# First context block in halves ahead of the tokens, and the last sums of the first attention placed ahead of other steps

## The reference

```
x = x + L0_xattn(layernorm(x), ctx)     # the setup and the first attention
x = x + L0_ffn(layernorm(x))            # shared experts and top 2 of 8
x = x + L1_xattn(layernorm(x), ctx)
x = x + L1_ffn(layernorm(x))

L0_xattn(q_feat, kv):                   # HIDDEN = 128
  Q = q_feat @ Wq;  K = kv @ Wk;  V = kv @ Wv
  ctx = softmax(Q K^T / sqrt(128)) @ V
  out = ctx @ Wo + bo + q_feat
  out = out @ Wfc
  return layernorm(out) * gamma + beta
```

## Time and profile before

| | us |
|---|---|
| median of 3 runs | 1042.13 (1041.17 to 1043.61) |
| profiled execution | 1041.9 |
| its span | 1040.1 |

### The profile page before, as it was taken

One profiled execution on the slowest core, in us unless ns is written; L12 is line 12 of the kernel. 1 busy time (PEld: TensorE's weight loads), 2 busy tenths in 40 slices (PEclk: granted clock), 3 DMA queues, 4 the chain that ended last, 5 costly groups with the idle time before them and its releaser, 6 DMA issues. The chain is left out here.

```text
span 1040.1 us, 18454 instructions
## 1 busy us (share of the span) xinstructions
PE 985.0 (95%) x6808; PEld 907.8 (87%) x6808; DVE 685.7 (66%) x1629; ACT 511.5 (49%) x1044; POOL 403.6 (39%) x631
## 2 busy tenths in 40 slices
PE   6999999699899999989989999999999999999996
PEld 5899998588899999988778889999998999999985
DVE  7577787568588888765675454455445676677664
ACT  5446666432477777753435333333334444444442
POOL 5514445507233443415632000000014767768651
PEclk9999999999999999999999999999999999999997
DMA  7200000101388888824213300000000111101000
GB/s 231 82 1 1 1 2 1 62 21 62 125 292 261 262 257 254 256 85 127 64 52 122 72 1 21 2 1 1 2 1 11 26 26 32 32 21 27 21 11 16
DMA packets 56878, 76.51 MB, mean 74 GB/s; under 512 B 5536, under 2 KB 37408, under 8 KB 56800
## 3 DMA queue, kind: packets, MB, share of 16 engines
q1 hardware_dynamic: 40480, 51.61, 16.0%
q0 software_dynamic: 15648, 22.81, 7.6%
q10 hardware_dynamic: 672, 1.05, 0.3%
HBM read 61.43 MB, written 14.02 MB: 73 GB/s over the span
## 5 line engine op out<-in xcount | busy, mean ns | idle before, releaser
L2472 DVE TENSOR_TENSOR XT_lo<-bank,XT_lo 128x512 fp32r<-128x512 f32 x116 | 73.3, 633 | 79.0 <-ACT XT_lo L2132 79.0
L43 PE MATMUL bank<-V_hi,XT_lo 128*128 128x256 f32 x416 | 123.6, 297 | 1.2 <-DVE XT_lo L2472 1.2
L2132 ACT ACTIVATE XT_lo<-bank 128x512 fp32r<-128x512 f32 x116 | 63.9, 553 | 120.1 <-PE bank L1839 119.5
L45 PE MATMUL bank<-V_hi,XT_lo 128*128 128x256 f32 x416 | 117.2, 282 | 0.0
L44 PE MATMUL bank<-V_lo,XT_lo 128*128 128x256 f32 x416 | 116.9, 281 | 0.0
L2477 DVE TENSOR_REDUCE part<-wide 128x1 f32<-128x402 f32 (+1 forms) x116 | 72.4, 624 | 39.7 <-PE wide L45 37.8
L43 PE MATMUL wide<-expert_w_hi,XT_hi 128*128 128x402 f32 (+2 forms) x236 | 93.5, 396 | 4.3 <-issue 2.4
L45 PE MATMUL wide<-expert_w_hi,XT_hi 128*128 128x402 f32 (+2 forms) x236 | 87.6, 371 | 0.0
L44 PE MATMUL wide<-expert_w_lo,XT_hi 128*128 128x402 f32 (+2 forms) x236 | 87.3, 370 | 0.0
L43 PEld LDWEIGHTS bank<-V_hi,XT_lo 128*128 128x128 f32 x416 | 78.3, 188 | 4.6 <-DVE XT_lo L2472 2.9
L44 PEld LDWEIGHTS bank<-V_lo,XT_lo 128*128 128x128 f32 x416 | 78.9, 190 | 0.4
(11 more groups left out here) (499 smaller groups left out, 3270.8 us busy)
## 6 DMA issues: line engine op xcount, KB each, us to landing
sraw<-w1T SPq DMA_DIRECT2D x13, 512.0 KB, 5.1
sraw<-w3T SPq DMA_DIRECT2D x13, 512.0 KB, 5.1
sraw<-w2T SPq DMA_DIRECT2D x13, 512.0 KB, 5.5
sraw_odd<-w1T SPq DMA_DIRECT2D x12, 512.0 KB, 4.8
sraw_odd<-w3T SPq DMA_DIRECT2D x12, 512.0 KB, 5.0
sraw_odd<-w2T SPq DMA_DIRECT2D x12, 512.0 KB, 5.1
XT_hi<-queries POOLq DMA_DIRECT2D x16, 256.0 KB, 3.2
routed_results<-rys POOLq DMA_DIRECT2D x15, 256.0 KB, 4.8
```

The costliest lines, as they stand in the source:

```text
L43: pe.matmul(out, wh, xh, start=first, stop=False)
L45: return pe.matmul(out, wl, xh, start=False, stop=last)
L2132: act.activation(weights(g, nk, 0), transposed(g, nk), ACT.Copy).then_inc(sem["high"], 1)
L2472: dve.tensor_tensor(weights(g, nk, 1), transposed(g, nk), weights(g, nk, 0).bitcast(F32), ALU.subtract).then_inc(sem["low"], 1)
```

## The change

In the setup the first context block is loaded, made into a high and a low part and multiplied in two halves of 256 columns. Both halves are issued by ACT, ahead of tokens 0, and the load of the whole block is gone from SP. On DVE the low parts of the weights and of the two halves now stand ahead of `statistics(0)`, and `statistics(1)` stands behind `normalise(0)` and the low part of `Wq`. In the first attention `split(14)` stands on POOL ahead of the second `inverse(12)`, and, for the tile step i = 15, `finish(13)` on DVE ahead of the statistics of tile 11's residual.

```diff
@@ first attention, POOL
                     for i in range(3, nq + 2):
-                        split(i - 3)
+                        if i <= nq:
+                            split(i - 3)
                         if real(i - 4):
                             add(i - 4)
                         inverse(i - 3, MV, RSTD, SHIFT, stat1, inv1)
+                        if i == nq:
+                            split(LAST - 1)
                         if real(i - 4):
                             inverse(i - 4, MV2, R2, H2, stat2, inv2)
@@ first attention, DVE
+                        if i == LAST:
+                            finish(i - 2)
                         if real(i - 4):
                             partial(i - 4, X, residual, stat2)
-                        if real(i - 2):
+                        if real(i - 2) and i < LAST:
                             finish(i - 2)
@@ setup, SP
                     weight("L0_xattn_Wv", lda)
-                    context(0)
                     weight("L0_xattn_Wq", ldq)
@@ setup, ACT
                 def _(act):
+                    for h, sem in enumerate((ldc_first, ldc[0])):
+                        act.dma_start(ctf[:, :, first_half(h)], A["ctxT"].rearrange("(c p) n -> p c n", p=P)[:, :, first_half(h)])\
+                           .then_inc(sem, 16)
                     act.dma_start(X[:, 0:4 * D].rearrange("p (i d) -> p i d", d=D),
...
-                    context_high(0)
+                    for h, sem in enumerate((ldc_first, ldc[0])):
+                        act.wait_ge(sem, 16)
+                        act.activation(CT_hi[:, :, first_half(h)], ctf[:, :, first_half(h)], ACT.Copy).then_inc(ctx_high, 1)
                     normalise(0)
@@ setup, DVE
+                    first_weights(0, slice(nq, na))
+                    for h in range(2):
+                        x = first_half(h)
+                        dve.wait_ge(ctx_high, h + 1)
+                        dve.tensor_tensor(CT_lo[:, :, x], ctf[:, :, x], CT_hi[:, :, x].bitcast(F32), ALU.subtract).then_inc(ctx_low0, 1)
                     statistics(0)
-                    first_weights(0, slice(nq, na))
-                    context_low(dve, 0)
-                    statistics(1)
                     normalise(0)
                     first_weights(1, slice(0, nq))
+                    statistics(1)
                     low(0)
@@ setup, PE
+                            if b == 0:
+                                for h in range(2):
+                                    pe.wait_ge(ctx_low0, h + 1)
+                                    x = first_half(h)
+                                    for c in range(DC):
+                                        m = mm3(pe, bank[:, x], kh[:, c, :], kl[:, c, :], CT_hi[:, c, x], CT_lo[:, c, x],
+                                                h == 0 and c == 0, h == 1 and c == DC - 1)
```

More of the change, by code:

```diff
@@ L2813, in build @@
                 ldc = sems(ctx, "ldc0 ldc1 ldc2 ldc3")
+                (ldc_first,) = sems(ctx, "ldc_first")
                 (first_high, first_low, second_high, second_low, ctx_high, ctx_low0, ctx_low, fold_high, fold_low, folded, fold_kept,
@@ L2855, in context_low, with first_half @@
                     x = ctx_cols(b)
-                    eng.wait_ge(ctx_high, b + 1)
-                    eng.tensor_tensor(CT_lo[:, :, x], ctf[:, :, x], CT_hi[:, :, x].bitcast(F32), ALU.subtract)\
-                       .then_inc(ctx_low if b else ctx_low0, 1)
+                    eng.wait_ge(ctx_high, b + 2)
+                    eng.tensor_tensor(CT_lo[:, :, x], ctf[:, :, x], CT_hi[:, :, x].bitcast(F32), ALU.subtract).then_inc(ctx_low, 1)
+                def first_half(h):
+                    return slice(256 * h, 256 * h + 256)
                 @blk.sync
@@ L3095, in unit @@
                         elif kind == "k":
-                            if b:
-                                pe.wait_ge(ctx_low, b)
[L3098 to L3103, removed]
+                            if b == 0:
[5 more added lines that the diff above has]
+                                                h == 0 and c == 0, h == 1 and c == DC - 1)
+                            else:
+                                pe.wait_ge(ctx_low, b)
+                                x = ctx_cols(b)
+                                for c in range(DC):
+                                    m = mm3(pe, bank[:, 0:x.stop - x.start], kh[:, c, :], kl[:, c, :], CT_hi[:, c, x], CT_lo[:, c, x],
+                                            c == 0, c == DC - 1)
                         elif kind == "v":
```

## The result

| | before | after |
|---|---|---|
| median of 20 runs | 1041.62 us (1038.54 to 1045.23) | 1045.67 us (1042.95 to 1051.3) |
| profiled execution | 1041.9 | 1043.3 |
| its span | 1040.1 | 1041.5 |
| first score matmul (the setup's end) | 41.84 | 46.92 |
| first waiting matmul of the experts | 206.84 | 211.38 |

The changed kernel is slower: the ratio is 1.0049, with a 95% interval of 1.0035 to 1.0062, or 3.6 to 6.5 us. I had forecast 1043.5 and no change that can be told. The median, 1045.67, lies just outside the range given, and within 0.6 us of the rival in which the clock stays low, 1045.1.

What follows compares the result with a forecast made beforehand. TensorE, busy 95% of the span, was taken as the bound. Setup + 2.2, split - 0.9 and finish(13) + 0.1 gave + 1.4 us: 1043.5 for the median, range 1041.3 to 1045.6.

Steps and rivals of the forecast that it cites:

- the rival in which the clock stays low: Setup, turn(0) to turn(1): PE stays at the low rate, costing 3.9 us in place of 2.3; 1045.1 us, chance 0.32.
- that of PE's clock: Setup, unit 1 and turn(1): fast rate returns after the new gap at an uncertain time; 2.3 us later taken.
- The third case: Setup: fast rate not before unit 1's end at 20.1, and turn(1) takes 1.91 in place of 1.06; 3.9 us.
- three cases: Setup, fast rate up before PE's restart, 5.6 us after it, or not before unit 1's end: 1.9, 2.4, 3.9 us.
- the 0.1 that I took for an earlier start: Setup loads: Wv may land ahead of the second half, so ACT's chain starts up to 0.6 us sooner; 0.1 taken.
- Unit 0 earlier, nobody to use it: Setup: PE's first matmul at 7.7 in place of 9.5, 1.8 us earlier, with no user before turn(0).
- the loads' step: Setup: new load order costs nothing, tokens in by 7.0 to 7.5; ends 0.6 us sooner or 0.5 later.
- the upper bound of 8.75: Setup: tokens' landing if Wq and all of tokens(1) went ahead, making the chain 0.5 us later.
- `turn(0)` at 13.2: Setup, PE: first transposes start at 13.2, not 12.20, because the tokens' statistics stand behind both halves on DVE.
- The queue behind each wait: Setup: statistics(1) waits behind normalise(0) and the split of Wq, so turn(1) can start at 19.0, 1.9 us later.
- The setup's sum: Whole setup: + 2.3 - 0.1 = + 2.2 us, with ends + 1.3 and + 4.4.
- The attention: First attention's end: moving split(14) gains 0.9 us, finish(13) costs 0.1, between 0 and 0.28.

Runs made afterwards that it cites:

- both edits together: Changed kernel with statistics(1) back ahead of normalise(0) and 14 unused matmuls behind unit 0, timed against the kernel before: 1041.51 us, ratio 1.0001.
- the last kernel with filling: Halves with before's load and DVE orders, only split(14) moved, plus six unused matmuls between unit 0 and turn(0), against the kernel before: 1044.51 us, ratio 1.001.

## Why the prediction was wrong

The step that failed is that of PE's clock: "I take 2.3, between the first two, since some of the early work may count". It didn't. The third case, the clock low until the end of unit 1, came true in all three profiles of the changed kernel, and in all nine of kernels whose unit 0 was in halves and had nothing put between it and `turn(0)`, whatever the loads and DVE's order. In the five with before's unit 0 and nothing added on PE the rate rose between the middle of `turn(0)` and the ninth matmul of unit 1, 3.6 to 6.0 us behind PE's first matmul: the 5.6 that I took as fixed is one value of a wide range. I had three cases from one row's spacing, and chose a middle value; the cases were 1.9, 2.4 and 3.9, and the rival had the right one. Of the 2.9 us by which the setup's 5.1 exceeds my 2.2, this step is 1.6 (3.9 in place of 2.3). The later start of `turn(0)`, 14.40 and not 13.2, is 1.2, and the 0.1 that I took for an earlier start is the rest. So the rival's time came so near in part by luck: its setup term, 3.9, was 1.2 too small as well.

Point by point:

- Unit 0 earlier, nobody to use it: right, and by more (6.86, not 7.7), since `Wv` landed ahead of the halves: the lower end named in the loads' step.
- The loads "cost nothing": wrong. The tokens landed at 8.95, past even the upper bound of 8.75, where I took 7.0 to 7.5. What I kept as the worst case, `Wq` and tokens 1 ahead of or beside them, is what SP's rows show (issued from 1.79 and 2.29); no run holds SP back to prove it. Both ends of the loads' step came true at once: `Wv` sooner, which helps only unit 0, and the tokens later, which hits `turn(0)`.
- `turn(0)` at 13.2: it was 14.40. Of the 1.2 us, 0.67 are the tokens, 0.24 the inverse (`SHIFT` took 2.36 from the statistics' end and not 2.12), 0.1 the statistics, and the rest the waits between the engines.
- The queue behind each wait, and so `turn(1)` late by itself: right. The normalised tokens were there at 19.94; with the 0.1 us that lay between ACT and PE at `turn(0)` (14.26, 14.40) `turn(1)` could have started at 20.1, 2.9 us later than before, where I had 1.9.
- The setup's sum: 2.9 for the tokens, 1.1 for the slow unit 1 behind them (21.16 in place of 20.1), 0.87 for `turn(1)` itself (1.93 for 1.06) and 0.2 in unit 2 make the 5.1 measured, against 2.2 and an upper end of 4.4. The terms don't simply add: with the tokens early again the slow clock alone holds `turn(1)` at 21.41, with the clock high through both turns the late tokens alone put `turn(1)` at 20.64 and brought a new low stretch behind it, and only both edits together give 2.6 to 4.0 us.
- PE's longest gap behind `turn(1)` is 1.7 us, not 0.7: the wait at a branch just ahead of the first score matmul (L2803 before), which I left out. It is 1.68 in both kernels and changes nothing in the sum.
- The attention: right. The split escaped the weights' subtraction (0.46 us), the join's wait of 1.37 went, and `turn_tokens(12)` gained 0.9, as taken. `finish(13)` cost 0.29 at the join of tile 13, against 0.1 with an end at 0.28. Net 0.5 to 0.9 over the profiles, against 0.8. The Trainium skill's exclusive lock ("SBUF — State Buffer", section "SBUF: two separate sides") fits as to who waits: the split's subtraction started at 188.30, ahead of DVE's at 188.36, and it was DVE's that grew, from 1.22 to 1.47; `R`, started at 188.84 beside the rest of it, took 1.08. The size fits less well: held until the split's end at 188.76, DVE's would have grown by 0.40, and it grew by 0.25.

The Trainium skill, "TensorE: Matmul & The Clock Gate", Part 1, spoke for the rival, and the changed kernel's trace sides with it: the rate, up at 9.7 behind unit 0's work, fell in the gap, at 13.1, ahead of `turn(0)`. The same fall stands there with `statistics(1)` back (13.7) and with the tokens' load first (15.0, where `turn(0)` starts at 14.96). But the gap isn't the whole of it. In the other five of the nine that had nothing ahead of unit 0 there is no fall: the rate never rose before unit 2, with a gap of 4.65 to 4.99 us or of 0.72 to 0.75. That a rule speaks for the costliest case should have set the value, not the chance alone.

By position the change costs 5.0 to 6.7 us in the setup and gives 0.5 to 0.9 in the attention, and the timed 3.6 to 6.5 agrees with that. A further 0.7 to 1.0 us seems to come back far behind, at a branch of PE near 463 us, told below.

What stays open: what it is in unit 0 that decides the clock (its 256 columns, its earlier start, or the idle time behind it; each of the nine profiles has more than one of these), and what decides whether the clock falls in the experts (260 to 300 us, 580 to 600 us), which parts the executions of the last kernel with filling by some 5 us, more than this change costs.

## What to carry to other kernels

When a transfer or a step is put first, look for what PE needs second: here the wait that shrank had nobody to use it, and all that stood behind the newly first steps became late. Where the array's rate hasn't risen yet, price each new pause at the low rate for the whole of the next stage, from a row at the low rate, not at a value between the cases. And when two causes end at nearly the same time, undo both together before saying that either is harmless. Where a gain seen by position is missing from the median, compare the granted clock of the executions, and of the same stretches elsewhere in the kernel, before doubting it.

## What the runs showed of the hardware

PE waits at a branch near 463 us (L846), where its code goes on in another block. Here are the rows of before and of after:

```profile
463.48 0.47 PE L43 MATMUL bank<-XT_hi,expert_w_hi 128*128 128x512 f32 x1 [2.91 <-PEq L846]
```

```profile
466.88 0.56 PE L43 MATMUL bank<-XT_hi,expert_w_hi 128*128 128x512 f32 x1 [1.96 <-PEq L846]
```

The wait is 2.66 to 3.01 us in the five profiles of kernels with PE's instructions as before, and 1.96 to 1.98 in every kernel with more of them in the setup, be it halves, filling or identity products. So a few more instructions 420 us earlier move it by 0.7 to 1.0 us. Why, these runs don't tell.

Two more: behind a row of 24 transposes of the identity (1.58 to 6.96) PE's rate was up at its next matmul, at 8.51, while over unit 1's 24 matmuls of 128 columns at 0.21 us spacing, 5.1 us in all, it didn't rise in any of nine profiles. And where DVE and POOL worked side by side here, the one that started second paid: 0.25 us for DVE's subtraction at 188.36, behind the split's, and then 0.9 us for POOL's `R` at 188.84, behind that (1.08, where its median is 0.21). Before, it was POOL's power that paid (1.61, where its median is 0.56).
